# A transformer block on one core: maxima split in four steps, the router's small operations dealt out differently, the last expert's output added in PSUM

## The reference

```python
Q, K, V = x @ qw, x @ kw, x @ vw          # 16 heads of 8, rope on Q and K
score = Q K^T / sqrt(8), causal; score - max; softmax
x = layernorm(x + (softmax(score) @ V) @ ow)
logits = x @ router_w + router_b          # 4 experts
probs = softmax(logits); the top 2, renormalised to sum 1 -> gates
h = silu(x @ w1[e]) * (x @ w3[e])
x = layernorm(x + sum_e gates[e] * (h @ w2[e]))
```

## Time and profile before

| | |
|---|---|
| median of 3 runs | 401.43 us (399.75 to 402.37) |
| the profiled execution | 401.07 us |
| its span | 399.3 us |
| TensorE busy | 370.5 us, 93% |
| VectorE busy | 318.5 us, 80% |
| ScalarE busy | 248.0 us, 62% |
| GpSimd busy | 202.2 us, 51% |
| attention | up to about 244 us of the span |
| units of the experts | about 244 to 391 us |
| tail | about 391 to 399.3 us |

### The profile page before, as it was taken

One profiled execution on the slowest core, in us unless ns is written; L12 is line 12 of the kernel. 1 busy time (PEld: TensorE's weight loads), 2 busy tenths in 40 slices (PEclk: granted clock), 3 DMA queues, 4 the chain that ended last, 5 costly groups with the idle time before them and its releaser, 6 DMA issues.

```text
span 399.3 us, 7150 instructions
## 1 busy us (share of the span) xinstructions
PE 370.5 (93%) x2282; PEld 191.2 (48%) x2304; DVE 318.5 (80%) x971; ACT 248.0 (62%) x348; POOL 202.2 (51%) x267
## 2 busy tenths in 40 slices
PE   7897979999999999999999889999999999999992
PEld 3442222332323323232232324888688868867881
DVE  2877999899898999989999652567878778785755
ACT  1361527687877878778787787556456545645560
POOL 7056578652524525244351513675567466636661
PEclk9999989999999999999999999999999999999996
DMA  7582110476342233322413003002030002003000
GB/s 223 180 234 52 36 22 25 97 217 210 66 112 45 52 98 79 90 49 56 100 29 78 8 10 103 27 7 54 2 105 29 0 20 88 27 0 106 2 27 28
DMA packets 50052, 27.85 MB, mean 70 GB/s; under 512 B 31099, under 2 KB 45627, under 8 KB 50014
## 3 DMA queue, kind: packets, MB, share of 16 engines
q1 hardware_dynamic: 47118, 25.48, 23.7%
q10 hardware_dynamic: 2896, 1.90, 1.7%
HBM read 18.49 MB, written 7.64 MB: 65 GB/s over the span
## 4 chain that ended last, share of the span: by engine, by line
PE 65%; DVE 19%; issue 7%; ACT 3%; DMA 2%; POOL 2%; POOLq 0%; SPq 0%; ACTq 0%; DVEq 0%
PE o_bank L1310 13%; PE bank L1374 10%; PE bank L1269 9%; PE t_bank L1374 8%; PE t_bank L1387 8%; PE t_bank L1292 7%; PE small_bank L1269 4%; DVE maxima L1008 4%; DVE x_tw L1004 3%; DVE mg_t L1004 2%; PE t_bank L1218 2%; ACT num L818 1%; DMA xT<-in_x_feat 1%; DVE x_w L1004 1%; DVE num L1137 1%
## 5 line engine op out<-in xcount | busy, mean ns | idle before, releaser
L818 ACT ACTIVATE num<-t_bank 128x1024 f32<-128x1024 f32 (+2 forms) x160 | 141.8, 941 | 56.9 <-PE t_bank L1292 56.8
L721 POOL TENSOR_TENSOR hid_lo<-num,q_op 128x512 fp32r<-128x512 f32 x63 | 82.4, 1307 | 56.2 <-ACT q_op L873 56.2
L691 POOL TENSOR_SCALAR_AFFINE_SELECT num<-num 128x512 f32<-128x512 f32 x64 | 40.1, 636 | 90.9 <-ACT num L818 89.3
L1310 PE MATMUL o_bank<-num,v_op 128*32 128x512 f32 (+3 forms) x768 | 78.8, 496 | 0.9
L873 ACT ACTIVATE q_op<-num 128x512 fp32r<-128x512 f32 x64 | 40.5, 633 | 50.3 <-DVE num L1137 49.5
L1269 PE MATMUL bank<-k_op,q_op 128*128 128x512 bf16 (+7 forms) x233 | 65.2, 328 | 3.2 <-DVE maxima L1004 1.4
L1008 DVE TENSOR_REDUCE maxima<-bank 128x1 f32<-128x512 f32 x90 | 59.9, 686 | 0.8 <-PE bank L1269 0.4
L1292 PE MATMUL t_bank<-q_op,k_op 64*128 64x512 bf16 (+3 forms) x384 | 48.8, 330 | 2.8 <-ACT num L818 1.4
L1269 PEld LDWEIGHTS bank<-k_op,q_op 128*128 128x128 bf16 x254 | 20.9, 97 | 58.3 <-DVE maxima L1004 20.7
L1004 DVE CUSTOM_DVE_ANT_0 x_tw<-bank,resid 128x256 f32<-128x256 f32 (+7 forms) x100 | 43.2, 454 | 4.3 <-PE bank L1269 3.4
L1137 DVE TENSOR_TENSOR num<-t_bank,num 128x512 f32<-128x512 f32 x32 | 22.1, 692 | 23.7 <-ACT num L880 23.6
(11 more groups left out here) (153 smaller groups left out, 600.9 us busy)
## 6 DMA issues: line engine op xcount, KB each, us to landing
q_op<-q_scratch SPq DMA_DIRECT2D x64, 48.0 KB
k_op<-k_scratch SPq DMA_DIRECT2D x32, 96.0 KB, 2.3
w_raw<-in_w_all SPq DMA_DIRECT2D x6, 512.0 KB, 4.4
turns_sb<-gate_scratch SPq DMA_DIRECT2D x8, 256.0 KB, 3.9
num<-gate_scratch SPq DMA_DIRECT2D x8, 256.0 KB, 3.6
xT<-o_sb SPq DMA_DIRECT2D x32, 32.0 KB
x_res<-in_x_tok ACTq DMA_DIRECT2D x4, 256.0 KB, 2.8
rden_all<-rden_scratch SPq DMA_DIRECT2D x2, 512.0 KB, 4.4
```

Source lines behind the costliest of these rows:

```text
L691: pool.affine_select(out=tile, in_=tile, compare_op=ALU.is_ge, fill=0.0, base=0, pattern=[[0, GH], [1, P]], channel_multiplier=-1)\
L721: pool.tensor_tensor(hid_lo[:, m % HB, :], hid[:, m % HB, :], hid_hi[:, m % HB, :].bitcast(F32), ALU.subtract).then_inc(f_lo, 1)
L818: act.activation(num[:, t % PB, :, off:CH].rearrange("p (k i) t -> p i k t", i=2)[:, :, h:h + each, :], t_bank[k % TB][:, :, 0:each * (CH ...
L1310: ins = pe.matmul(o_bank[h * QD:(h + 1) * QD, off:CH], v_op[w][:, kt, h, :], num[:, t % PB, h, off:CH], start=kt == 0, stop=kt == TI * (c ...
```

## The change

1. `split_max` no longer negates. The filler rows of the keys are -1.0 instead of 1.0 and the maxima themselves are split: four operations instead of five.
2. The router's small operations are spread differently: step 9 keeps three operations, the others form steps 10, 11 and 12; tanh becomes step 13, the gates 14, their transposing 15. Two pairs of operations no longer wait between them. The tables place transposed input, logits and the small steps one unit earlier (TensorE's logits behind unit 12 instead of 13). The steps in `SHORT` stand directly behind the hidden product, before the expert's output product or sum. In the last attention stage steps 10 and 11 share one place.
3. In the last chunk the sum of the first three experts is multiplied by the identity into the banks 6 and 7 behind unit 16's output matmuls, leaving the accumulation open. The last expert's gated output is added by further matmuls with the identity. VectorE's two half sums go.

```diff
-C_STEPS = 16
-C_AT = [2 + 16 * r // 14 for r in range(C_STEPS)]
+C_STEPS = 15
+C_AT = [2 + 16 * r // 14 for r in range(C_STEPS + 1)]
+LAST_R = [(r,) for r in range(10)] + [(10, 11), (12,), (13,), (14,), (15,)]
...
-PE_NEXT = {1: 3, 6: 10, 8: 13, 14: 18}
-DVE_NEXT = {0: 1, 1: 3, 2: 4, 3: 5, 5: 8, 7: 11, 9: 13, 10: 14, 11: 15, 13: 17, 14: 18}
-ACT_NEXT = {7: 11, 8: 12, 12: 16}
+PE_NEXT = {1: 3, 6: 10, 8: 12, 15: 18}
+DVE_NEXT = {0: 1, 1: 3, 2: 4, 3: 5, 5: 8, 7: 10, 9: 12, 10: 13, 11: 14, 12: 16, 14: 17, 15: 18}
+ACT_NEXT = {7: 10, 8: 11, 13: 17}
 POOL_NEXT = {3: 6}
+SHORT = (9, 10, 11, 12, 14)
...
-            pool.memset(k_op[0][:, :, :], 1.0).then_inc(ops_filled, 1)
+            pool.memset(k_op[0][:, :, :], -1.0).then_inc(ops_filled, 1)
...
-                then(pool.tensor_scalar(neg_max[:, :, :], top, -1.0, None, ALU.mult), 1)
-                then(pool.tensor_copy(part[:, 0, :, :], neg_max[:, :, :]), 2)
-                then(pool.tensor_tensor(rest[:, :, :], neg_max[:, :, :], part[:, 0, :, :], ALU.subtract), 3)
-                then(pool.tensor_copy(part[:, 1, :, :], rest[:, :, :]), 4)
-                then(pool.tensor_tensor(part[:, 2, :, :], rest[:, :, :], part[:, 1, :, :], ALU.subtract), 5)
+                then(pool.tensor_copy(part[:, 0, :, :], top), 1)
+                then(pool.tensor_tensor(rest[:, :, :], top, part[:, 0, :, :], ALU.subtract), 2)
+                then(pool.tensor_copy(part[:, 1, :, :], rest[:, :, :]), 3)
+                then(pool.tensor_tensor(part[:, 2, :, :], rest[:, :, :], part[:, 1, :, :], ALU.subtract), 4)
...
-                    then(dve.tensor_tensor(gt[:, :, :, :], a, z, ALU.is_gt), k + 2)
+                    dve.tensor_tensor(gt[:, :, :, :], a, z, ALU.is_gt).then_inc(c_step, 1)
                     then(dve.tensor_tensor(ge[:, :, :, :], a, z, ALU.is_ge), k + 3)
-                    then(dve.tensor_tensor(gt_f, gt_f, upper, ALU.mult), k + 4)
                 if r == 10:
+                    dve.tensor_tensor(gt_f, gt_f, upper, ALU.mult).then_inc(c_step, 1)
                     then(dve.tensor_tensor(ge_f, ge_f, lower, ALU.mult), k + 5)
                     then(dve.tensor_tensor(gt_f, gt_f, ge_f, ALU.add), k + 6)
-                    then(dve.tensor_reduce(rank[:, :, :], gt[:, :, :, :], AX.X, ALU.add), k + 7)
-                    then(dve.tensor_reduce(top[:, :], logits[:, :, :], AX.X, ALU.max), k + 8)
                 if r == 11:
+                    dve.tensor_reduce(top[:, :], logits[:, :, :], AX.X, ALU.max).then_inc(c_step, 1)
+                    then(dve.tensor_reduce(rank[:, :, :], gt[:, :, :, :], AX.X, ALU.add), k + 8)
                     then(dve.tensor_scalar(chosen[:, :, :], rank[:, :, :], 1.5, None, ALU.is_lt), k + 9)
+                if r == 12:
                     then(dve.tensor_tensor(logits[:, :, :], logits[:, :, :],
...
-                    for k, half in enumerate(halves(ch, e)):
+                    for k, half in enumerate(halves(ch, e) if (ch, e) != (CHUNKS - 1, E - 1) else ()):
                         dve.wait_ge(f_eo, 2 + ch * E + e + 1 + k)
...
+            def unit(n, i):
+                later = n >= UNITS and i + 1 < CHUNKS
+                if later:
+                    experts_hid(i + 1, n - UNITS)
+                experts_hid(i, n)
+                steps = next_steps(n, i, DVE_NEXT)
+                for ch, r in steps:
+                    if r in SHORT:
+                        between(ch, r)
+                if later:
+                    experts_out(i + 1, n - UNITS)
+                experts_out(i, n)
+                for ch, r in steps:
+                    if r not in SHORT:
+                        between(ch, r)
...
-                if n == TR_STEP:
+                if ch < CHUNKS - 1 and n == TR_STEP:
                     pe.wait_ge(f_z, ch + 1)
-                    if ch == CHUNKS - 1:
-                        pe.wait_ge(g_copied, CHUNKS)
+                    pe.wait_ge(f_y, (ch + 1) * E)
+                    for i in range(0, CH, P):
+                        ins = pe.transpose(bank[6][:, i:i + P], sum_t[:, i:i + P], ident[:, :])
+                    ins.then_inc(f_tr, 1)
+                if ch == CHUNKS - 1 and n == UNITS:
+                    pe.wait_ge(f_z, ch + 1)
+                    pe.wait_ge(g_copied, CHUNKS)
+                    pe.wait_ge(f_y, (ch + 1) * E - 1)
+                    for i in range(0, CH, P):
+                        pe.matmul(bank[6 + i // (CH // 2)][:, i:i + P], sum_t[:, i:i + P], ident[:, :],
+                                  start=i % (CH // 2) == 0, stop=False)
+                if ch == CHUNKS - 1 and n == TR_STEP:
                     for k, half in enumerate(halves(ch, E - 1)):
-                        pe.wait_ge(f_y, (ch + 1) * E + k)
+                        pe.wait_ge(f_eo, 2 + ch * E + E + k)
                         for i in range(half.start, half.stop, P):
-                            ins = pe.transpose(bank[6 + k][:, i:i + P], sum_t[:, i:i + P], ident[:, :])
+                            ins = pe.matmul(bank[6 + k][:, i:i + P], gated[:, (E - 1) % 2, i:i + P], ident[:, :],
+                                            start=False, stop=i + P == half.stop)
                         ins.then_inc(f_tr, 1)
```

More of the change, by code:

```diff
@@ L79 @@
 PB = 4
-C_STEPS = 16
-C_AT = [2 + 16 * r // 14 for r in range(C_STEPS)]
+C_STEPS = 15
+C_AT = [2 + 16 * r // 14 for r in range(C_STEPS + 1)]
+LAST_R = [(r,) for r in range(10)] + [(10, 11), (12,), (13,), (14,), (15,)]
+assert len(LAST_R) == C_STEPS
 PROJ_FIRST = 4
@@ L323, in transformer_block @@
         maxima = sb("maxima", [P, 2, NPR, S // QB])
-        neg_max, rest = sb("neg_max", [P, NPR, NB]), sb("rest", [P, NPR, NB])
+        rest = sb("rest", [P, NPR, NB])
         max_part = [sb(f"max_part{c}", [P, PARTS, NPR, NB], BF16) for c in range(NC)]
@@ L633, in _ @@
             pool.memset(q_flat[1][:, :].bitcast(F32), 0.0).then_inc(ops_filled, 1)
-            pool.memset(k_op[1][:, :, :], 1.0).then_inc(ops_filled, 1)
+            pool.memset(k_op[1][:, :, :], -1.0).then_inc(ops_filled, 1)
             pool.memset(minus_half[:, :], -0.5).then_inc(ops_filled, 1)
@@ L643, in split_max @@
             def split_max(s, c):
-                first = 5 * (NC * s + c)
+                first = 4 * (NC * s + c)
                 top = maxima[:, 0, :, c * NB:(c + 1) * NB]
@@ L677, in stage @@
                         lay_v((n + 1) % NG, (n + 1) // NG, u)
-                    if step[0] == "C":
-                        between(0, step[1], first=True)
+                    if step[0] == "C" and step[1] < C_STEPS:
+                        for r in LAST_R[step[1]]:
+                            between(0, r, first=True)
                     if step[0] == "E":
@@ L841, in stage @@
                     if step[0] == "C" and step[1] == 12:
-                        between(0, 0, 0, step[1])
+                        between(0, 0, 0, 13)
                     if step[0] == "E":
@@ L861, in between @@
                     act.activation(x1_tw[:, :], turns[:, :], ACT.Copy).then_inc(c_x1s, 1)
-                if r == 12:
+                if r == 13:
                     act.wait_ge(c_top, 1 + ch + 1)
@@ L1021, in stage @@
                         dve.tensor_copy(max_rows[c][:, :], ring(s, step)[0:NPR * PARTS * NB, 0:P]).then_inc(job_read, 1)
-                    if step[0] == "C":
-                        between(0, step[1], first=True)
+                    if step[0] == "C" and step[1] < C_STEPS:
+                        for r in LAST_R[step[1]]:
+                            between(0, r, first=True)
                     if step[0] == "E":
-                        experts(0, step[1])
-                        for next_step in next_steps(step[1], 0, DVE_NEXT):
-                            between(*next_step)
+                        unit(step[1], 0)
             for s in range(GROUPS):
@@ L1118, in between @@
                                              logits[:, :, :], ALU.mult, ALU.add).then_inc(c_top, 1)
-                if r == 13:
+                if r == 14:
                     dve.wait_ge(c_tanh, ch + 1)
@@ L1126, in between @@
                                       ALU.mult).then_inc(c_done, 1)
-                if r == 14:
+                if r == 15:
                     dve.wait_ge(g_turned, ch + 1)
@@ L1130, in between, with experts_hid @@
                     dve.tensor_copy(gates_t[:, :], bank[7][0:E * TI, 0:P]).then_inc(g_copied, 1)
-            def experts(ch, n):
+            def experts_hid(ch, n):
                 if n < UNITS:
@@ L1138, in experts, with experts_out @@
                                       ALU.mult).then_inc(f_hid, 1)
+            def experts_out(ch, n):
                 if ch == CHUNKS - 1 and n == UNITS:
@@ L1183, in _ @@
             for n in range(E_LAST, HEAD):
-                experts(0, n)
-                for step in next_steps(n, 0, DVE_NEXT):
-                    between(*step)
+                unit(n, 0)
             for i in range(0, CHUNKS - 1):
```

(8 more changed lines are left out.)

## The result

| | before | changed |
|---|---|---|
| median of 7 runs each | 401.43 us | 397.07 us |
| profiled execution, its span | 401.07, 399.3 us | 396.48, 394.7 us |

The ratio is 0.9893, 95% interval 0.9867 to 0.9919: 4.3 us faster, with 3.3 to 5.3 inside the interval. The forecast was 397.2. One run of the changed kernel (689 us) and one of a later kernel (`f3_best`, 1418 us) were far slower than all others and are outside the comparisons.

The account below looks back on a forecast made before the run. TensorE, busy 93% of 399.3 us, was taken as the bound, so only its idle places pay. -4.15 - 0.55 + 0.5 = -4.2 us gives 397.2 us against the 401.43 median; 8 in 10 from 395.6 to 399.3.

Parts of the forecast that it names:

- Gating: Router at chunk boundaries: removing three VectorE-GpSimd collisions each (L1103, L1106, L1115) and transpose waits saves 4.15 us (2.0 to 4.6).
- the window: Between the hidden product's end and GpSimd's next subtraction: 0.74 us in which three small operations start without collision.
- Split: Attention stages: one operation fewer in splitting the maxima, 0.32 us off the chain; 0.55 us saved in all (0 to 1.9).
- The stage at 76: Middle attention stage whose row matmul is already early; it gains nothing and shows 0.31 us there becoming 0.13 behind.
- the stage that gives it back to the DMA: Attention stage at 101 us: TensorE waits 0.19 us for the rows' DMA, so its 0.13 gain is given back.
- Tail: Program's end, last expert added in PSUM: first gated half 1.12 us later, 0.65 saved after; net 0.5 us slower.
- the stop for expert 2's sum: Behind unit 16's output matmuls: TensorE idles 0.8 us for VectorE's sum, then spends 0.89 us on eight matmuls.
- collisions moved: Rival at chunk boundaries: GpSimd still overlaps in two groups each, half of the 4.15 us stays; 399.3 us, chance 0.15.
- split in full: Rival in the attention stages: the shorter split saves 1.9 us instead of 0.55; 395.8 us, chance 0.12.
- tail pays: Rival at the end: the eight matmuls fall in free TensorE time, tail 0.7 us shorter; 396.0 us, chance 0.08.
- SyncE gives back more than the one stage: Rival in attention stages: rows' DMAs keep stages in step, a later one loses a further 0.5; 398.3 us, chance 0.07.
- the router's chain holds TensorE: Rival at unit 12: TensorE's step 8 waits for ScalarE's copy, 2.7 us a chunk; 405.3 us, chance 0.04.

Follow-up runs that it names:

- f3_best: Changed kernel with the unused 64-byte `neg_max` kept and the three-expert sum in two halves behind units 17 and 18: ratio 0.9879, second time 0.9867, 395.17 us.
- f4_short_behind: Changed kernel with unused 64-byte `neg_max` kept and `SHORT` empty, so small groups stand behind the expert's output product and sum: ratio 0.9866, experts 137.89 us.
- the padded one: Changed kernel with the unused 64-byte tile `neg_max` kept in its place in SBUF: ratio to before 0.9886, experts 137.90 us.
- g3_late: Changed kernel with unused 64-byte `neg_max` kept, steps at the unit places of before, new groups and short-first order kept: 398.46 us (one execution), experts 137.89.

## Why the prediction was right

- **Gating**: mechanism and place right, for all three operations, and so is the order of events in the window. The rule that whoever is issued first keeps the port, which the rows before showed from one side only, has its other side in the last section. 4.15 us were forecast, 4.55 came with the tiles in their old places. Of the whole change only 3.05 arrived; the missing term is the place of `hid_lo`, of which the prediction knew nothing. "The negated filler of the key rows is the same memset and costs nothing" was right, but the tile that went with the negation cost 1.5 us. The window was given the credit. f4_short_behind shows that it isn't needed once the groups are spread; the spread alone, at the old places and without the window, was not run.
- **Split**: 0.55 forecast, 0.73 measured over the stages, less 0.13 in the last. The three stages gave 0.12 each against 0.13 forecast. The last one, put at 0.15, gave 0.46 less 0.13, about the whole 0.32 of the operation; the stage at 100 us lost 0.10 where it was put at nothing. The stage at 76 as a measure for the others was right to 0.01 us (24.42), and the stage that gives it back to the DMA was named rightly. Not foreseen: the halved clock in the last stage of some executions.
- **Tail**: +0.5 forecast, +0.64 measured; the stop for expert 2's sum, 0.87 us of it idle, was put right, and the gated half follows the last matmul by 0.50 instead of 0.43. TensorE kept the full clock through its last matmuls (granted clock 1.00 from 386 to 389 us), as forecast.
- **Sum**: measured segments without the start give -3.0, the timed runs -4.3 (3.3 to 5.3), and what makes up the difference in them is open. The forecast of -4.2 met the time with a gating term too large by 1.1 in the changed kernel and a difference of the start that it didn't have. That it fell within 0.2 us is in good part luck.
- **Rivals**: collisions moved (no), split in full (no), tail pays (no; it costs), SyncE gives back more than the one stage (no), the router's chain holds TensorE (no: no wait on `x_tw` in the expert phase).

## What to carry to other kernels

Where two engines share a lock, look for the time in which the other is sure to be idle, but first count what the deadline can bear: here a single collision of 1.2 us a boundary cost nothing, while one in each of three units in a row was behind most of the 4.55 us. A wait put into an in-order queue is paid by everything behind it, so give new matmuls the place where the engine already waits. When a tile is removed, hold the others' places until the time is measured: here a shift of 64 bytes hid a third of the gain.

## What the runs showed of the hardware

The place of one tile, `hid_lo`, sets the mean pitch of the matmuls of the expert phase, and not only at the one in nine that reads it: 0.2285 to 0.229 us in the old place (nine profiles), 0.2314 to 0.2315 at 64 bytes less (three), 0.2281 with only this tile in its old place, 0.2297 at 64 bytes more. These are means over 515 to 527 differences of neighbouring starts between 0.20 and 0.26 us, from the first expert matmul to the mark in the last unit, at a granted clock of 1.0. In the changed kernel the difference is longest behind a `q_op,w_hi` matmul of the first layer (0.237 against 0.228 in the padded one). Why stays open.

Between VectorE and GpSimd the one that starts second is held up the other way round too: where VectorE's sum of two SBUF tiles is under way first, the sum takes its usual 0.69 us and GpSimd's subtraction 1.55 instead of 1.30 (`g3_late`):

```profile
281.38 0.69 DVE L1167 TENSOR_TENSOR num<-num 128x512 f32<-128x512 f32 x1
281.68 1.55 POOL L724 TENSOR_TENSOR hid_lo<-num,q_op 128x512 fp32r<-128x512 f32 x1 [0.73 <-ACT q_op L876]
```

In the changed kernel the same subtraction takes 1.30 us at 276.34, where VectorE's product, under way for the same 0.30 us, has one input in PSUM.
